# Last routed layer of a four-layer network: another ranking, bf16 products, and first products ahead of the ranking

## The reference, cut to what matters

```python
prob = softmax(xf @ router_w.T + router_b)            # xf: normalised x, n x 128; prob: n x 16
_, idx = top_k(prob, 4)                               # ties: the lower index first
mask = zeros((n, 16), bool).at[arange(n)[:, None], idx].set(True)
h = einsum('nd,ibd->nib', xf, w1b) + b1b              # 16 blocks of 32 hidden units
h = relu(where(mask[:, :, None], h, 0))
y = einsum('nib,dib->nd', h, w2b) + b2
x = x + y
```

## Time and profile before

| | |
|---|---|
| Runs, median (lowest to highest) | 4396.57 us (4387.61 to 4402.43) |
| Span of the profiled execution, first to last instruction | 4385.4 us |
| Busy: PE, DVE, ACT, POOL | 91%, 78%, 63%, 61% of the span |
| Mean granted clock of TensorE | 0.939 of full speed |
| Largest group: L483, POOL, in the attention stages | 1631.5 us busy |

### The profile page before, as it was taken

The page is one execution under the profiler, slowest core; times in us unless marked ns, Lnnn a source line. Parts: engine busy times, 40 slices in busy tenths (PEclk is TensorE's granted clock), DMA queues, the critical chain, the costliest instruction groups (busy, mean ns, idle before and its releaser), DMA issues. The chain is left out here.

```text
span 4385.4 us, 103422 instructions
## 1 busy us (share of the span) xinstructions
PE 4003.2 (91%) x40427; PEld 2873.2 (66%) x40427; DVE 3408.8 (78%) x6672; ACT 2756.6 (63%) x5342; POOL 2685.0 (61%) x2445
## 2 busy tenths in 40 slices
PE   6999999888879999999799999996996899999977
PEld 4777777754545777777467777774664577777753
DVE  6999998667788888888688888876555888888833
ACT  4787877554446777777377777761441677777721
POOL 3888888656664767777367677771002476767730
PEclk9999999889989999999699999995997999999986
DMA  4333333124341111111111111100001111111100
GB/s 112 94 90 96 87 99 89 53 62 119 117 118 43 51 40 51 49 46 30 33 41 46 53 37 54 44 23 19 1 1 32 45 46 46 46 54 42 34 12 9
DMA packets 113025, 237.08 MB, mean 54 GB/s; under 512 B 15000, under 2 KB 53160, under 8 KB 111160
## 3 DMA queue, kind: packets, MB, share of 16 engines
q1 hardware_dynamic: 112088, 230.40, 18.3%
q10 hardware_dynamic: 448, 0.06, 0.0%
HBM read 165.23 MB, written 50.26 MB: 49 GB/s over the span
## 5 line engine op out<-in xcount | busy, mean ns | idle before, releaser
L483 POOL TENSOR_TENSOR wst<-wst 125x384 bf16<-125x384 f32 (+1 forms) x1536 | 1631.5, 1062 | 841.3 <-ACT wst L681 776.7
L681 ACT ACTIVATE wst<-ps 125x448 f32<-125x448 f32 x3072 | 1498.1, 543 | 406.9 <-PE ps L164 397.9
L738 DVE TENSOR_TENSOR wst<-wst 125x512 bf16<-125x512 f32 (+1 forms) x1536 | 1403.9, 915 | 270.5 <-ACT wst L681 254.9
L164 PE MATMUL ps<-big,cx 128*125 128x448 bf16 (+1 forms) x6144 | 1435.1, 355 | 0.0
L164 PEld LDWEIGHTS ps<-cx,wst 125*128 125x128 bf16 x23040 | 1105.4, 98 | 354.7 <-issue 60.2
L164 PE MATMUL ps<-cx,wst 125*128 125x65 bf16 (+2 forms) x23040 | 1202.3, 204 | 27.8 <-POOL wst L483 13.3
L164 PEld LDWEIGHTS ps<-big,cx 128*125 128x125 bf16 (+1 forms) x6144 | 814.6, 137 | 287.2 <-issue 23.1
L164 PE MATMUL ps<-cx,big 128*128 128x500 bf16 (+1 forms) x2688 | 713.2, 318 | 27.7 <-DVE wst L708 14.2
L705 DVE CUSTOM_DVE_ANT_0 wst<-ps,wst 128x500 bf16<-128x500 f32 x896 | 603.8, 674 | 166.3 <-PE ps L164 122.5
L630 ACT ACTIVATE wst<-ps 128x500 bf16<-128x500 f32 x896 | 530.1, 592 | 226.9 <-PE ps L164 173.5
L708 DVE TENSOR_REDUCE wst<-ps 128x1 f32<-128x500 f32 x896 | 600.5, 670 | 36.3 <-PE ps L164 27.1
(11 more groups left out here) (213 smaller groups left out, 4158.2 us busy)
## 6 DMA issues: line engine op xcount, KB each, us to landing
cx<-ctxT SPq DMA_DIRECT2D x96, 375.0 KB, 3.5
cx<-ctxN SPq DMA_DIRECT2D x64, 377.9 KB
cx<-in_ctxN SPq DMA_DIRECT2D x64, 375.0 KB
cx<-ctxT SPq DMA_DIRECT2D x96, 187.5 KB, 3.8
ctxN<-cx SPq DMA_DIRECT2D x32, 377.9 KB
ynN<-cx SPq DMA_DIRECT2D x32, 377.9 KB
cx<-ynN SPq DMA_DIRECT2D x32, 377.9 KB
cTs<-in_ctxT SPq DMA_DIRECT2D x64, 187.5 KB, 6.8
```

The source lines that it names most:

```text
L164: return t.matmul(o, l, r, start=start, stop=stop, skip_group_check=True)
L483: g.tensor_tensor(pl[r][0:KP, at:], pf[r][0:KP, at:], pf[r][0:KP, at:].bitcast(BF16)[:, 1::2], ALU.subtract).then_inc(s["plp"], 1)
L681: e.activation(pf[T % 3][0:KP, cols], bank(2 + n2 % 3, 448)[0:KP], ACT.Exp, scale=scale).then_inc(s["ev"], 1)
L738: v.tensor_tensor(pl[r][0:KP, 0:to], pf[r][0:KP, 0:to], pf[r][0:KP, 0:to].bitcast(BF16)[:, 1::2], ALU.subtract).then_inc(s["pl"], 1)
```

## The change

Only the last layer is changed in what its engines do. The four semaphores that count memsets (`oz`, `zt`, `zh`, `rz`) become one, `clear`, with offsets, and the waits on them stay where they are; `xsh` and `xsl` are new.

- Ranking. Instead of `dve_rank`, DVE writes the normalised probabilities into `probs` (20 wide, the last four set to -2), and for each of the 16 column groups takes the eight largest with `v.max`; one memset puts -2 in place of the fifth to the eighth; `v.match_replace` then goes over `probs` for each group and writes -1 over the first match of each of the eight values; one compare with -1 gives `sel16`. That is 34 calls in place of six. Table `tri16` and its load are gone.
- Flags and spread. `selT` and `spread_b` are bf16 and 128 partitions deep, zero outside the first 16. POOL clears them and the pads of `probs` ahead of its two powers, and copies `spread` into `spread_b` behind them.
- First product in bf16. ACT casts `f1` and `xT` to bf16 (`f1hw`, `x4h`), POOL subtracts to get the rest (`f1lw`, `x4l`), and PE adds three products: high x high, high x low, low x high.
- Order. The first products of chunk 0 and their relus are written ahead of the transposes of the flags; the transposes use other banks.

The core of the diff (`max`, `memset`, `match_replace` are single calls of the language; `last_releases` is unchanged):

```diff
@@ -932,8 +933,8 @@
         def pool_f0(g, w):
             wait_cross(w, 0)
             for i, o in enumerate(oo):
-                g.memset(o, 0.0).then_inc(s["oz"], 1)
-                w.wait_ge(s["oz"], i + 1)
+                g.memset(o, 0.0).then_inc(s["clear"], 1)
+                w.wait_ge(s["clear"], i + 1)
             pool_norm(g, w, 1)
             pool_fold(g, w, 1)
             for c in range(4):
...
@@ -1687,8 +1688,8 @@
 
         def pool_mlp(g, w, i, norm):
             for c, h in enumerate(hid):
-                g.memset(h, 0.0).then_inc(s["zh"], 1)
-                w.wait_ge(s["zh"], 2 * i + c + 1)
+                g.memset(h, 0.0).then_inc(s["clear"], 1)
+                w.wait_ge(s["clear"], CLEAR_MLP + 2 * i + c + 1)
             pool_norm(g, w, norm)
 
         def pe_mlp(t, w, i, at, brow):
...
@@ -1786,29 +1787,49 @@
         rw = wst[:, 0:16]
         f1 = wst[:, 128:640].rearrange("p (m n) -> p m n", m=4)
         f2 = wst[:, 640:1152].rearrange("p (m n) -> p m n", m=4)
-        tri16 = wst[:, 1152:1152 + 256].rearrange("p (i j) -> p i j", i=16)
         spread = wst[0:16, 1408:1920].rearrange("p (m n) -> p m n", m=4)
         fb = wst[:, 1920:1924]
         rbias = wst[:, 1928:1944]
-        g16 = [big[:, 2048 * i:2048 * i + 2048].bitcast(BF16).rearrange("p (b i j) -> p b i j", b=NP, i=16) for i in range(2)]
+        probs, kept = (big[:, 448 * i:448 * i + 320].rearrange("p (b e) -> p b e", b=NP) for i in range(2))
+        mx8 = big[:, 320:448].rearrange("p (b e) -> p b e", b=NP)
+        spread_b = wst[:, 2048:2304].bitcast(BF16).rearrange("p (m n) -> p m n", m=4)
+        f1hw, f1lw = (wst[:, 2304 + 256 * i:2560 + 256 * i].bitcast(BF16) for i in range(2))
+        f1h, f1l = (v.rearrange("p (m n) -> p m n", m=4) for v in (f1hw, f1lw))
+        x4h, x4l = (w32[:, 1024 * i:1024 * i + 1024].bitcast(BF16) for i in range(2))
         lg16 = big[:, 12544:12800].rearrange("p (b e) -> p b e", b=NP)
         sel16 = big[:, 12800:13056].rearrange("p (b e) -> p b e", b=NP)
-        selT = big[0:16, 13056:13056 + 2048]
+        selT = big[:, 13056:13056 + 1024].bitcast(BF16)
         hid4 = [big[:, 16384:18432], big[:, 18432:20480]]
         rel = [big[:, 8192 + 448 * i:8192 + 448 * i + 448] for i in range(4)]
 
+        SPLIT_F4 = 0
+
         def sp_f4(y, w):
             wait_mlp(w, 1)
-            for o, name in ((rw, "routerT"), (f1, "w1T"), (f2, "w2T"), (tri16, "tri16"), (spread, "spread"), (fb, "f1b"),
+            for o, name in ((rw, "routerT"), (f1, "w1T"), (f2, "w2T"), (spread, "spread"), (fb, "f1b"),
                             (crow[:, :], "f2b"), (rbias, "routerb")):
                 y.dma_start(o, a[name]).then_inc(s["w"], 16)
 
         def pool_f4(g, w):
             wait_mlp(w, 1)
             for i, h in enumerate(hid4):
-                g.memset(h, 0.0).then_inc(s["rz"], 1)
-                w.wait_ge(s["rz"], i + 1)
+                g.memset(h, 0.0).then_inc(s["clear"], 1)
+                w.wait_ge(s["clear"], CLEAR_F4 + i + 1)
+            for i, (o, value) in enumerate(((probs[:, :, 16:20], -2.0), (selT, 0.0), (spread_b, 0.0))):
+                g.memset(o, value).then_inc(s["clear"], 1)
+                w.wait_ge(s["clear"], CLEAR_F4 + i + 3)
             pool_norm(g, w, 13)
+            w.wait_ge(s["w"], 800)
+            g.tensor_copy(spread_b[0:16], spread).then_inc(s["clear"], 1)
+            w.wait_ge(s["clear"], CLEAR_F4 + 6)
+            w.wait_ge(s["xsh"], SPLIT_F4 + 1)
+            g.tensor_tensor(f1lw, f1.rearrange("p m n -> p (m n)"), f1hw, ALU.subtract).then_inc(s["xsl"], 1)
+            w.wait_ge(s["xsl"], SPLIT_F4 + 1)
+            for g4 in range(4):
+                cols = slice(512 * g4, 512 * g4 + 512)
+                w.wait_ge(s["xsh"], SPLIT_F4 + g4 + 2)
+                g.tensor_tensor(x4l[:, cols], xT[:, cols], x4h[:, cols], ALU.subtract).then_inc(s["xsl"], 1)
+                w.wait_ge(s["xsl"], SPLIT_F4 + g4 + 2)
 
         def last_releases():
             r = []
...
@@ -1822,17 +1843,29 @@
             wait_mlp(w, 1)
             pe_turn(t, w, xn, s["xn"], 208, 1)
             wait_turned(w, 6)
-            w.wait_ge(s["w"], 816)
+            w.wait_ge(s["w"], 800)
             for p in range(NP):
                 o = bank(4)[:, 16 * p:16 * p + 16]
                 r = mm(t, o, xT[:, 128 * p:128 * p + 128], rw, True, True)
             r.then_inc(s["gm"], 1)
-            w.wait_ge(s["rt"], 12)
+
+            def up(c, m):
+                o = bank((1 + 12 * c + 2 * m) % 8, 448)
+                mm(t, o, f1h[:, m, :], tok8(x4h, c), True, False)
+                mm(t, o, f1h[:, m, :], tok8(x4l, c), False, False)
+                mm(t, o, f1l[:, m, :], tok8(x4h, c), False, True).then_inc(s["rh"], 1)
+
+            w.wait_ge(s["xsh"], SPLIT_F4 + 5)
+            w.wait_ge(s["xsl"], SPLIT_F4 + 5)
+            for m in range(4):
+                up(0, m)
+            w.wait_ge(s["rt"], 40)
             for g4 in range(4):
                 for q in range(4):
-                    r = t.transpose(bank((5 + g4) % 8)[0:16, 128 * q:128 * q + 128], sel16[:, 4 * g4 + q, :], idf[:, :])
+                    r = t.transpose(bank((2 + 2 * g4) % 8)[0:16, 128 * q:128 * q + 128], sel16[:, 4 * g4 + q, :], idf[:, :])
                 r.then_inc(s["ctm"], 1)
             w.wait_ge(s["cta"], 8)
+            w.wait_ge(s["clear"], CLEAR_F4 + 6)
             freed = last_releases()
             for c in range(4):
                 hv = hid4[c % 2].rearrange("p (m n) -> p m n", m=4)
...
@@ -1840,10 +1873,11 @@
                     i = 12 * c + 2 * m
                     if i >= 8:
                         w.wait_ge(s[freed[i - 8][0]], freed[i - 8][1])
-                    mm(t, bank((1 + i) % 8, 448), f1[:, m, :], tok8(xT, c), True, True).then_inc(s["rh"], 1)
+                    if c:
+                        up(c, m)
                     if i >= 8:
                         w.wait_ge(s[freed[i - 7][0]], freed[i - 7][1])
-                    mm(t, bank((2 + i) % 8, 448), spread[:, m, :], tok8(selT, c), True, True).then_inc(s["rsm"], 1)
+                    mm(t, bank((2 + i) % 8, 448), spread_b[:, m, :], tok8(selT, c), True, True).then_inc(s["rsm"], 1)
                 for q in range(4):
                     i = 12 * c + 8 + q
                     w.wait_ge(s[freed[i - 8][0]], freed[i - 8][1])
...
@@ -1870,11 +1904,19 @@
             w.wait_ge(s["rt"], 4)
             v.reciprocal(small[:, 32:32 + NP], small[:, 16:16 + NP]).then_inc(s["rt"], 1)
             w.wait_ge(s["rt"], 5)
-            v.tensor_tensor(lg16, lg16, per_row(small[:, 32:32 + NP], 16), ALU.mult).then_inc(s["rt"], 1)
-            w.wait_ge(s["w"], 816)
+            v.tensor_tensor(probs[:, :, 0:16], lg16, per_row(small[:, 32:32 + NP], 16), ALU.mult).then_inc(s["rt"], 1)
             w.wait_ge(s["rt"], 6)
-            dve_rank(v, w, s["rt"], 6, lg16, NP, 16, 4, tri16, sel16, *g16)
-            w.wait_ge(s["rz"], 2)
+            for p in range(NP):
+                v.max(mx8[:, p, :], probs[:, p, 0:16]).then_inc(s["rt"], 1)
+            w.wait_ge(s["rt"], 22)
+            v.memset(mx8[:, :, 4:8], -2.0).then_inc(s["rt"], 1)
+            w.wait_ge(s["rt"], 23)
+            w.wait_ge(s["clear"], CLEAR_F4 + 5)
+            for p in range(NP):
+                v.match_replace(out=kept[:, p, :], in_to_replace=mx8[:, p, :], in_values=probs[:, p, :],
+                                imm_value=-1.0).then_inc(s["rt"], 1)
+            w.wait_ge(s["rt"], 39)
+            v.tensor_scalar(sel16, kept[:, :, 0:16], -1.0, None, ALU.is_equal).then_inc(s["rt"], 1)
             for c in range(4):
                 hv = hid4[c % 2].rearrange("p (m n) -> p m n", m=4)
                 for m in range(4):
...
@@ -1895,17 +1937,29 @@
             act_turned(e, w, 6, xT, 10)
             w.wait_ge(s["rt"], 3)
             e.activation(lg16, lg16, ACT.Exp).then_inc(s["ge"], 1)
+            w.wait_ge(s["w"], 800)
+            e.activation(f1hw, f1.rearrange("p m n -> p (m n)"), ACT.Copy).then_inc(s["xsh"], 1)
+            wait_turned(w, 6)
+            for g4 in range(4):
+                cols = slice(512 * g4, 512 * g4 + 512)
+                e.activation(x4h[:, cols], xT[:, cols], ACT.Copy).then_inc(s["xsh"], 1)
+
+            def relu(c, m):
+                i = 12 * c + 2 * m
+                w.wait_ge(s["rh"], 4 * c + m + 1)
+                if c:
+                    w.wait_ge(s["rp"], 4 * (c - 1) + m + 1)
+                e.activation(rel[m], bank((1 + i) % 8, 448), ACT.Relu, bias=fb[:, m:m + 1]).then_inc(s["rr"], 1)
+
+            for m in range(4):
+                relu(0, m)
+            w.wait_ge(s["clear"], CLEAR_F4 + 5)
             for g4 in range(4):
                 w.wait_ge(s["ctm"], g4 + 5)
-                e.activation(selT[:, 512 * g4:512 * g4 + 512], bank((5 + g4) % 8)[0:16, :], ACT.Copy).then_inc(s["cta"], 1)
-            w.wait_ge(s["w"], 816)
-            for c in range(4):
```

(8 more changed lines are left out.)

13 lines of the change are left out of this document (7 added, 6 removed), and 8 rows, old and new, of the table s.

## The result

Four runs of the changed kernel: median 4337.04 us (4334.22 to 4344.11). Four of the kernel before, beside them: 4396.8 (4387.61 to 4402.43). Ratio 0.9865, interval 0.9851 to 0.988. In a later session with more runs the changed kernel took 4335.57 (4 runs) and the one before 4388.56 (15 runs), ratio 0.9882 [0.9869, 0.9896], which is 53 us.

The account below looks back on a forecast made before the run. A single file of waits in the last 125 us, PE busiest, clock partly at 0.50. Summed backwards from 4378.7, the layer would end at 4338.0: saving 40.7, 4396.6 - 40.7 = 4355.9 us; range 4340 to 4372, likeliest case 4350 to 4362.

Parts of the forecast that it names:

- the base of the sum: Saving summed in the profiled execution (span 4385.4 us), then taken off the median of three runs, 4396.57.
- step 6: Clock's rise: low through chunk 0's q half, back about 5 us into chunk 1, which takes 12.35 us.
- step 2: Transposes start 7.7 us earlier, set by casts, subtractions and twelve early products; ranking, 4.3 to 8.7, ends before.
- Step 3: Transposes of the flags and their copies: 4.26 us as before, so 0 saved.
- Step 4: Chunk 0's first half: 3.3 us instead of 15.1, 11.8 earlier; its q half unchanged at 10.04, low clock.
- Step 1: POOL's added memsets ahead of the norm's power: 2.5 us later, a bf16 element costing the full price.
- Step 5: Chunks 1 to 3 with bf16 products: first half 4.4 us at high clock (was 8.26), 7.2 low (was 14.95).
- The tail of relu and multiply: End of a chunk's first half: last multiply waits for relu, 1.4 us after the last first product.
- the main case: Clock low at chunk 0's q half, back during chunk 1: saving 40.7 us, 4355.9 us; chance 0.46.
- rival A: Clock rises within chunk 0's early products and stays: saving 49.8 us, 4346.8 us; chance 0.25.
- D: DVE's search instructions slow, 4.42 us a pair in the ranking: 4417 us, slower than before; chance 0.03.

Follow-up runs that it names:

- e2_after_again: The changed kernel run again without any edit, in a later session: 4335.57 us, ratio 0.9882 to the kernel before.
- e4_no_reorder: The changed kernel with chunk 0's first products and relus back behind the transposes and their copies: 4336.0 us, ratio 0.9882 to the kernel before.
- e6_delay1: The kernel before with only the new ranking, plus one old whole-tile comparison on DVE (4.42 us, result unused): 4369.87 us, ratio 0.9951.
- e8_delay3: The kernel before with only the new ranking, plus three old whole-tile comparisons on DVE (4.42 us each, results unused): 4387.61 us, ratio 0.9968.
- e5_fill: The kernel before with 100 unused bf16 products of 448 columns on PE ahead of the transposes: 4378.78 us, ratio 0.9973.
- e10_no_pad: The changed kernel with the bf16 spread products reading 16 partitions again instead of 128: 4354.4 us, ratio 0.9901 to the kernel before.
- e7_delay2: The kernel before with only the new ranking, plus two old whole-tile comparisons on DVE (4.42 us each, results unused): 4393.12 us, ratio 0.9995.
- e3_rank_only: The kernel before with only the new ranking added: 4344.92 us, ratio 0.9902.
- e15_rank_again: The kernel before with only the new ranking, the same text run a second time: 4345.1 us (4341.48 to 4375.43), ratio 0.9918.
- e12_best: The changed kernel with ACT's casts ahead of the exponential and POOL's powers first, its clears behind the subtractions: 4331.27 us, ratio 0.985 to the kernel before.

## Why the prediction was right in kind and too small

**The account.** 40.7 us were predicted. 59.8 measured are: 40.7, plus 5.1 by which the layer beat the sum (45.8), plus 3.6 ahead of it, less 0.1 in the output, which makes the 49.3 between the spans; and 10.5 because the two medians lie further apart than the two profiled executions. (Span plus the 1.8 us that lie around it puts the execution of before at 4387.2, 9.6 below its median; that of after was 0.9 above its own.)

**The step that failed is the base of the sum: "so I carry the difference over, not the sum".** It took 40.7 us off 4396.57, the median of three executions, while all its rows come from one that took 4387.2 (the 11 us named there set a span against times; by times it is 9.4). Off that execution the same sum gives 4346.5, and the same range, 9.4 lower, 4331 to 4363, would have held the result. What the runs showed in its place: 4387 to 4390 as the median in four samples of 11 to 35 runs, 4398 in one of nine, and 4389.0 in the middle of all 87. The profiled execution was a usual one, and the three runs beside it lay high. So the 10.5 are for the most part the draw of four runs, and a gain of 52 to 53 us is what the larger samples bear out. That the layer of the kernel before took 124.5 us in one trace and 140.5 in the next shows that the loss to the clock differs between executions; whether a median execution loses more than the one that I read, no run shows. The 3.6 us ahead of the layer belong to no edit that a trace shows: that stretch took 4254.2 and 4245.3 us in the kernel before, 4250.6 and 4242.9 in the changed one, and up to 4258.9 elsewhere. 14.1 of the 19.1 by which the saving was missed are in these two terms.

**The term that was mis-sized in the layer is step 6, the time of the clock's rise.** The other 5.1 us are 1.2 in step 2 and some 4 of the clock: 3.2 in steps 3 and 4, because it rose at 4283.4, behind the early products, which step 6 had called possible and left out of the sum; and 0.9 because it rose 3.1 us into chunk 1 and not 5.

**Step 1 held.** POOL's power starts 6.5 us into the layer, before 3.9: +2.6, predicted +2.5. A bf16 element cost what an f32 one does (2048 of them and the pads 2.01).

**Step 2 held in its order, and was 1.2 short.** The strand of casts, subtractions and early products set the start, as forecast: subtractions 6.15 us in all (6.05), twelve products 4.65 (4.5). The ranking took 4.8, in the forecast 4.3 to 8.7, near its low end: maxima 0.08 us apart, replacements 0.15. The transposes are 8.95 us earlier in the layer (7.7). The rest is the router products, 5.3 us instead of 7.0, at a clock that was high for part of them (0.67 in the mean), which no step foresaw and no edit explains; in e2_after_again, the same kernel, it was low there throughout.

POOL holding up DVE was priced at nothing in the sum, and it shows, small and nearly all on covered work. Beside POOL's two-input subtraction DVE's multiply by the reciprocal took 1.32 us, where the same one took 0.42 before; the compare took 0.77 (0.29 before):

```profile
4274.83 0.42 DVE L1873 TENSOR_TENSOR big<-big,small 128x256 f32<-128x256 f32 x1
```
The maxima, with one input each, were not held. The normalising took 4.48 beside POOL's cast of 0.60 against 4.19: 0.3 on the path. The Trainium skill, "SBUF — State Buffer", "Who interferes with whom", has a DVE instruction with two SBUF inputs contend with a POOL instruction that reads SBUF, and one with a single input outside the two-port modes not; the multiply and the maxima agree. The prediction gave that section's rule up to 1.2 us for the normalising, and a quarter of that was measured.

**Step 3: 2.99 us where 4.26 stood,** because the clock rose at 4283.4. **Step 4: first half 2.67 (3.3), q half 8.76 (10.04),** high until 4290.3, then low. **Step 5: 9.95 and 10.4 for chunks 2 and 3 (9.9, 10.4).** The tail of relu and multiply is in the chain at 4301.97 and 4302.71 as forecast. **Step 6: chunk 1 took 11.48 (12.35)**: the clock rose 3.1 us into it, not 5. So the main case's pattern, low at chunk 0's q half and back in chunk 1, is what happened, with some 4 us of it better than rated. It was not rival A: the clock did fall. (Rival A's pattern, one rise and no fall, is that of e4_no_reorder, without the early products.) D fell with the first row of MAX8: a pair of search instructions cost 0.23 us, not the 3.2 that it needed.

**Where the reason was wrong.** The prediction gave the gain to the ranking (step 2), to the order (step 4) and to bf16 (step 5), and the depth of the spread products, 128 rows instead of 16, entered only as something that lets the clock rise during chunk 1. It named the right condition and gave it no price of its own. The runs do: 34.7 us for depth alone, 42 to 44 for the ranking alone, 51.2 for both, by the medians nothing for bf16 and order. For bf16 step 5 counted 3.9 us a chunk at the high clock (first half 8.26 to 4.4). Measured from second half to second half it is 3.8 (13.76 to 9.95), of which 1.4 come by depth alone; the other 2.4 are in the traces, but set against the strand of casts and subtractions and the fall of the clock behind the early products they don't reach the medians. That the forecast lies in the right direction and near the right pattern is thus in part luck: what it credits with the gain is not what the runs credit.

**Open.** Two changes bring the clock back in the chunks, a ranking that leaves PE idle for 16 us less (7.5 for 23.3) and depth within the chunks. Depth did it in each of the traced executions, and no second group shows in 36 runs; the ranking alone did it in nine of twelve, by their times. What in an execution of e6_delay1 or e8_delay3 decides between its two groups, with the same instructions at the same places, no run shows; that two delays never had the fast group and three had it in four of ten argues against idle time as such. e5_fill shows one execution in which a clock already high was not enough. I have not tried other depths between 16 and 128.

## What to carry to other kernels

Where products of few rows sit between full ones in a stage whose granted clock reads 0.50 although TensorE is never idle, try zeros up to 128 rows before making anything cheaper: here two memsets and a copy brought 35 us by themselves, and 8 to 10 on top of the new ranking. Before a saving is worked out from one trace, compare that trace's time with the median and the spread, and subtract from the trace's own time; if the stage that is to be changed runs at either clock level from one execution to the next, work from several traces. And parts of a change that end the same loss don't add up: run each alone and both together.

## What the runs showed of the hardware

- Depth counts for the time of a product. At clock 1.00 f32 products of 448 columns followed each other in 0.75 us when all were 128 deep and in 0.95 when every second one was 16 deep. At 0.50, in e10_no_pad, the next bf16 product came 0.48 us after a 16-deep one; in the changed kernel, 0.37 after a 128-deep one:

```profile
4296.01 0.55 PE L164 MATMUL ps<-big,wst 16*128 16x448 bf16 x1
4296.49 1.30 PE L164 MATMUL ps<-xn,wst 128*128 128x448 bf16 x3
```
```profile
4298.53 0.58 PE L164 MATMUL ps<-big,wst 128*128 128x448 bf16 x1
4298.90 0.58 PE L164 MATMUL ps<-xn,wst 128*128 128x448 bf16 x1
```

  The Trainium skill, "TensorE: Matmul & The Clock Gate" ("Why this matters for your kernels"), has a single product 32 rows deep take the time of one 128 rows deep. The durations by themselves are near that; the spacing in a mixed row of them is not.
- A busy TensorE was at the low clock for all but some 7 us of 99 (96.88 us busy of 99.3 at 0.53, e7_delay2), and at the high one for 28 us with less of its time busy (25.41 of 28.0, changed kernel). Depth and type of the products differ between the two, but they alone don't decide either: the very products of e7_delay2 ran at 0.90 in e6_delay1 (61.34 busy of 64.4).
- One program has executions some 30 us apart. Of one such pair, e3_rank_only and e15_rank_again, both traces are there: the same instructions from transposes to output took 64.2 us at 0.90 and 91.1 at 0.59.
- POOL's memset costs by element: 2048 bf16 took 1.80 us in e12_best, as 2048 f32 did before (3.67 for two).
